# Two more 512-column matmuls in each part of the block builder of a four-layer graph network

## The reference

```
L0  attention with one head:  e = leaky(z @ w1 @ w2), softmax over the edges of a node,
    agg = segment_sum(a * h[src], dst);             relu(agg + h @ loop_weight)
L1  aggr = segment_sum(h[src] @ W_msg + b_msg, row); relu([h, aggr] @ W_upd + b_upd)
L2  twice: h = segment_sum((h * norm)[src] * w, dst) * norm;  mean of the three embeddings
L3  attention with 8 heads and self loops, then two layer norms around a small MLP
```

## Time and profile before

| what | value |
|---|---|
| median of three runs | 5580.41 us |
| the profiled execution, on the device | 5609.29 us |
| its span, first to last instruction | 5607.6 us |
| share of the span busy: TensorE, its weight loads, VectorE, ScalarE, GpSimd | 49, 39, 43, 8, 32% |
| mean granted TensorE clock over the span | 0.614 |
| block builder (first to last matmul of its parts) | 1596.2 to 2153.5 us |

### The profile page before, as it was taken

How to read it: one execution, slowest core, us unless ns; L and a number is a source line. 1 busy time by engine, 2 the same in 40 slices (tenths; PEclk the granted TensorE clock), 3 DMA queues, 4 the chain that set the end, 5 groups by cost and what they waited for, 6 DMA issues and landing times.

```text
span 5607.6 us, 46533 instructions
## 1 busy us (share of the span) xinstructions
PE 2765.6 (49%) x14416; PEld 2175.0 (39%) x14458; DVE 2436.0 (43%) x4207; ACT 473.0 (8%) x909; POOL 1797.6 (32%) x1742
## 2 busy tenths in 40 slices
PE   2085022122678885989898500004770001059995
PEld 1083000000157774979733400004660001059983
DVE  4068221111677776970101500006999800035565
ACT  0000000000022331003200100001220110000000
POOL 3705777777100001000000777771000077720000
PEclk8555555555555555989999655557995555555556
DMA  3102222222236665314476121110000123102210
GB/s 109 52 1 61 58 75 62 71 62 65 85 82 140 138 144 155 109 49 160 177 269 220 44 52 49 46 48 10 0 0 23 70 80 73 49 15 66 63 35 23
DMA packets 246489, 433.22 MB, mean 77 GB/s; under 512 B 140538, under 2 KB 142311, under 8 KB 231895
## 3 DMA queue, kind: packets, MB, share of 16 engines
q10 hardware_dynamic: 126001, 172.60, 12.0%
q1 hardware_dynamic: 64102, 198.46, 10.0%
q0 software_dynamic: 56256, 60.51, 5.8%
HBM read 280.32 MB, written 150.98 MB: 77 GB/s over the span
## 4 chain that ended last, share of the span: by engine, by line
PE 35%; issue 25%; another core or an unknown queue 17%; DVE 10%; POOL 9%; DMA 2%; ACT 1%; DVEq 0%; SPq 0%; ACTq 0%; POOLq 0%
POOL ring L652 8%; PE PS L1272 7%; PE PS L1196 5%; PE PS L1096 4%; PE PS L1098 4%; PE PS L989 3%; PE PS L1029 3%; PE PS L1167 3%; PE PS L992 2%; PE PS L1175 1%; DVE s_ring L1612 1%; DVE s_ring L1613 1%; PE PS L1270 1%; PE PS L1290 1%
## 5 line engine op out<-in xcount | busy, mean ns | idle before, releaser
L652 POOL DMA_INDIRECT ring<-d_h,idx_lin x1568 | 1579.1, 1007 | 598.6 <-issue 519.4
L1272 PE MATMUL PS<-arena,s_ring 128*128 x1968 | 432.5, 414 | 198.1 <-issue 198.1
L1096 PE MATMUL PS<-qa 128*125 128x150 bf16 x1050 | 412.3, 393 | 107.0 <-DVE arena L1662 46.1
L1929 DVE TENSOR_TENSOR big<-PS,big 128x800 f32<-128x800 f32 x196 | 193.8, 989 | 619.5 <-issue 335.7
L1272 PEld LDWEIGHTS PS<-arena,s_ring 128*128 128x128 f32 x1968 | 439.8, 330 | 9.2 <-issue 1.1
L1221 PE MATMUL PS<-big 128*125 128x128 bf16 x784 | 134.0, 300 | 618.5 <-issue 449.2
L1098 PE MATMUL PS<-qa 128*125 128x150 bf16 x1050 | 401.2, 382 | 0.0
L1059 PE MATMUL PS<-s_ring,arena 81*128 81x512 bf16 x196 | 121.6, 621 | 561.0 <-issue 353.3
L1221 PEld LDWEIGHTS PS<-big 128*125 128x125 bf16 x784 | 106.9, 209 | 664.8 <-issue 456.6
L671 POOL DMA_INDIRECT d_fa<-asd,start_i x25 | 50.2, 2010 | 889.5 <-DVEq L1323 882.2
L1231 PE MATMUL PS<-big,arena 125*128 125x200 bf16 x2352 | 271.6, 272 | 118.3 <-ACT arena L900 100.9
(11 more groups left out here) (445 smaller groups left out, 4572.2 us busy)
## 6 DMA issues: line engine op xcount, KB each, us to landing
big<-d_wgt SPq DMA_DIRECT2D x50, 1562.5 KB, 7.2
d_stash<-ring SPq DMA_DIRECT2D x196, 256.0 KB
arena<-d_stash ACTq DMA_DIRECT2D x196, 256.0 KB
big<-d_cnt SPq DMA_DIRECT2D x25, 1562.5 KB, 6.5
ring<-d_h,idx_lin POOLq DMA_INDIRECT x1568
d_cnt<-big ACTq DMA_DIRECT2D x13, 1562.5 KB, 5.5
d_wgt<-big ACTq DMA_DIRECT2D x13, 1562.5 KB, 15.7
d_cnt<-arena ACTq DMA_DIRECT2D x12, 1562.5 KB, 5.4
```

Of the source, the lines that this page charges most:

```text
L652: pool.indirect_dma_start(ring[:, HALF * h + s, :], None, table, bass.IndirectOffsetOnAxis(ap=idx_lin[:, CH * i + s:CH * i + s + 1], axis= ...
L1096: nc.tensor.matmul(bank(3 * half + s // 2, NP, 2 * CW, at), lhs, hot_step(half, s, W, 2 * CW), start=(s % 2 == 0), stop=False, skip_group_ ...
L1272: mm = nc.tensor.matmul(PS[:, bass.ds(place[s] + j % SUMS * BANK, D)], marks[:, j % 2, s, :], arena[:, bass.ds(at[s], D)], start=False, st ...
L1929: v_.tensor_tensor(picked.rearrange("p (s h k) -> p s h k", s=CB, h=H), free(PS[:, 0:1], [[BANK // 2, CB], [NB, H], [1, NB]], 2 * j * BANK ...
```

## The change

In `part_products`, behind the two matmuls of the second set (s = 1) and those of the fourth (s = 3), TensorE gets one more matmul. It has 128 rows, 128 stationary columns and 512 moving ones, all from the tile of ones, and writes the whole of bank 7, which nobody reads while the builder runs. It neither waits for a semaphore nor raises one. In 175 parts that makes 350 more matmuls.

```diff
@@ -1097,6 +1097,8 @@
                     mm = nc.tensor.matmul(bank(3 * half + s // 2, NP, 2 * CW, at + CW), lhs, hot_step(half, s, W + 2 * CW, 2 * CW),
                                           start=False, stop=False, skip_group_check=True)
+                    if s in (1, 3):
+                        nc.tensor.matmul(bank(7, P, BANK), ones_bf[:, 0:P], free(ones_bf[:, 0:1], [[0, 2], [1, 2 * P]]), start=True, stop=True)
                 mm.then_inc(S["part_done"], 1)
```

## The result

The changed kernel takes 5692.24 us (median of four runs, 5684.74 to 5696.41) against 5578.99 us before (four runs): 1.0194 times as long, with a 95% interval of 1.0173 to 1.0215. That is 113 us slower. 5710 us (+130) were forecast; the range of 5625 to 5745 holds the result.

The account below looks back on a forecast made before the run. The builder was taken to be bound by TensorE at the lower clock; 150.5 us for the extra matmuls less 21.0 us of waits gave +129.5 us, so 5580.4 + 129.5 = 5710 us, range 5625 to 5745 us.

Parts of the forecast that it names:

- The price of one matmul: Builder's parts: each extra matmul costs TensorE 0.43 us at the lower clock, 350 of them 150.5 us.
- The bounds of 0.35 and 0.52: Limits in us for each extra matmul: 122.5 us in all (5682 us) or 182 us (5741 us).
- rival D: Extra matmul's load is not hidden, or its bank or tile holds up the next: up to +161 us, 5741 us; chance 0.10.
- What it hides: Between parts: TensorE's 75 waits of 0.28 us for VectorE vanish, -21.0 us.
- VectorE's waits at L1650: In the builder: VectorE's waits for TensorE's L1098, 66.3 us before, would grow by over 100 us.
- What stays: The 3.8 us hole once a block, 96.0 us in all, stays; extra matmuls beside it are paid in full.
- rival C: In the parts: extra matmuls only fill TensorE's waits and cost nothing, +10 us or less; chance 0.05.
- The clock: TensorE's granted clock in the builder stays at the lower 0.50; given three chances in four.
- A: Builder: clock rises, strided matmuls get no faster; +56 us (5636 us) if up throughout, likelier some 5673 us; chance 0.15.
- B: A part's twelve matmuls: clock rises and they follow it; -58 us, 5522 us at the higher clock throughout; chance 0.08.
- The row that the prediction took for it: Look-up, L1221, strided: four matmuls take 0.43 us at the lower clock, 0.52 at the higher, so strided reads keep their pace.
- The span against the medians: Whole program: the median lies 28.9 us under the profiled execution of 5609.3 us; the same difference was set on the forecast.

Follow-up runs that it names:

- Experiment 10: The changed kernel with 256 columns in each extra matmul instead of 512; 5621.6 us in one run against 5577.3 us, builder 602.5 us.
- experiment 4: The changed kernel, two extra matmuls kept, the parts' matmuls reading neighbouring values for both operands (wrong sums); 3788 us against 3780, builder 516 us.
- experiment 2: The changed kernel with only the first extra matmul of each part, 175 in all; 3826.7 us against 3779.6 for the kernel before, 1.0129 times.
- experiment 9: The kernel before with eight extra matmuls behind each overflow of a block, none in the parts; 5579.82 us against 5577.32, 1.0004 times.
- experiment 1: The changed kernel with a 512-column matmul behind each of a part's six sets, 1050 in all; 4002 us in one run against 3780.
- experiment 5: The kernel before, unchanged, traced again beside the changed kernel; 5578.5 us, builder 557.4 us.
- experiment 7: The kernel before with only the 125 stationary columns read from neighbouring places (wrong sums); 5596 us in one run, builder 547.9 us.

## Why the prediction was right

**The price of one matmul.** Forecast 0.43 us from the steps of L0, measured 0.403 from its start to the next, which is 0.401 more than the builder's own step (0.202 + 0.403 - 0.204). That is 140 us in place of 150, the one term of the sum that was off by more than 1 us. The row of L0 was the right instruction with another follower. Experiment 10 splits it: 256 columns less cost 0.216 us less, which is 1.2 GHz, so what is missing is 0.026 us that belong to no column. It is missing where the follower reads 12 bytes apart, and not where it is packed (0.427 in experiment 4 at the lower clock) or in the steps of L0. The reason stays open. The bounds of 0.35 and 0.52, and with the latter rival D, are out.

**What it hides.** The waits went, as forecast: -21 us. (By the starts of the matmuls there were 76 of them, 21.7 us in all.) The full sum is 140.4 - 21.0 = +119.4 us, and the builder grew by 118.9 and 119.4. Experiments 2 and 10 show 20 to 21 us at other sizes. I had expected VectorE's waits at L1650 alone to grow by over 100 us, and that was wrong. They grew by 87, from 66.3 to 153.0 over the whole builder; another 31 us came at the overflow (32.3 to 63.2 us together).

**What stays.** The hole is 96.1 us as before, and experiment 9 shows that it could have held the matmuls for nothing (rival C had them in the parts, where it failed).

**The clock.** It stayed at 0.50 in the builder in both traces of the changed kernel. That was the likelier case of a judgement, three chances in four, and not a derivation; with six long matmuls in a part it was 0.91 (experiment 1). Rivals A and B needed it up. The experiments tell them apart all the same: A was the right mechanism (0.18 to 0.20 us at the higher clock in experiment 1, 0.204 in 9), B was not. The row that the prediction took for it, L1221, was weaker than it was read: its 0.52 us hold the 0.1 us of a first matmul behind a wait, and its 0.43 us at the lower clock are just the 512 columns of four matmuls. The look-up as a whole bears the reading out: between two starts of L1221 lie 0.114 us at the lower clock and 0.118 at the higher (medians).

**The span against the medians.** The profiled executions differ by 5687.2 - 5607.6 = 80 us only, 39 less than their builders. The rest lies where nothing was changed: the look-up took 1084 us in the trace before and 1072 after, the end of the program behind the steps of L3 190 and 180, the counting blocks of L1 221 and 214, the steps of L0 255 and 249. What makes these differ from one execution to the next was not followed up, but for the steps of L0 (last section). That profiled execution before was 29 us above its median, and the changed one was not. The builder's own +119 agrees with the medians (+113 and +120), so 5580 + 119 = 5699 would have been the better forecast of the same method.

## What to carry to other kernels

A matmul put in to keep TensorE's clock up cost its full length where TensorE was the engine that is late (70 us for the second of a part), and nothing where it waits (experiment 9): read first where the hole is. Before paying for the clock, look at whether the matmuls would follow it: their starts at the lower clock, against columns over 1.2 GHz, tell that from one row (0.204 us for 150 columns said no). And a stretch that gets shorter pays only if nothing on another engine was hidden behind it.

## What the runs showed that I had not expected

The clock in the steps of L0 came up at very different times with the same instructions: 14 us after their start in the trace before, 2.6 us in the one after, and 65 us in experiment 5, where TensorE was busy without a break all the while (in experiment 7 too it was 65 us). The stage takes 249 us in the changed kernel and 279 us there. Stretches of experiment 5, then of the changed kernel:

```profile
2216.30:2281.70 65.40, 65.40 (x284) 60.01 (x284) 40.66 (x122) 0.00 (x0) 0.00 (x0) 0.50 0.14 38
2281.70:2495.40 213.70, 213.70 (x1758) 197.68 (x1758) 206.31 (x688) 1.28 (x1) 0.00 (x0) 1.00 0.32 94
```
```profile
2337.20:2339.90 2.70, 2.70 (x14) 2.51 (x13) 2.70 (x12) 0.00 (x0) 0.00 (x0) 0.51 0.06 17
2339.90:2586.50 246.60, 246.60 (x2028) 228.06 (x2028) 238.89 (x799) 1.28 (x1) 0.00 (x0) 1.00 0.32 91
```

These 30 us are as much as the runs of the kernel before differ (5570 to 5605 us beside experiment 9). They are not all of it: the trace before is 6 us longer than that of experiment 5, though its steps of L0 are 24 us shorter. The builder took 557.3 and 557.4 us in the two, and that is why it is the better scale here.

And the same program takes 5579 or 3780 us. The difference lies wholly outside the builder. Between the first and the last start of their matmuls the histogram took 354 us in the trace before and 180 in experiment 2, the scoring of edges (L1052 to L1059) 1047 and 358, the look-up 1084 and 473, the steps of L3 770 and 549. In the scoring of the trace before VectorE stands idle for about 7 us ahead of one instruction in eight, 88 times and 597 us in all, while GpSimd's indirect DMAs run beside it; in experiment 2 it never waits 5 us there. The gathers themselves start 1.25 us apart in both (medians). So in the shorter program they are not done when the builder begins. First the trace before, then experiment 2:

```profile
903.18 0.74 DVE L1619 SCALAR_TENSOR_TENSOR s_ring<-qa,mix_id,PS 81x512 bf16<-81x512 uint8 x1 [6.87 <-remote]
```
```profile
449.33 0.73 DVE L1621 SCALAR_TENSOR_TENSOR s_ring<-qa,mix_id,PS 81x512 bf16<-81x512 uint8 x1
450.78 0.73 DVE L1621 SCALAR_TENSOR_TENSOR s_ring<-qa,mix_id,PS 81x512 bf16<-81x512 uint8 x1
```

What makes the one or the other stays open. Runs beside each other were always of one kind. The record has both kinds under the same chip number (4), 16 minutes apart, so it need not be the chip.
